# Transformer decoder layer, last stage: the output projection from f16 parts, and new instruction orders for four engines

## What is computed

```python
x = x + attention(layernorm(x)) @ Wo                       # 16 heads, short and long attention mixed
x = x + cross_attention(query=layernorm(x), memory=ctx)    # 8 heads, 77 memory rows, masked
x = x + fp4_linear(silu(fp4_linear(h, w_gate)) * fp4_linear(h, w_up), w_down)   # h = layernorm(x)
```

## Time and profile before

| | |
|---|---|
| median of 3 runs | 4975.11 us (4972.73 to 4979.94) |
| the profiled execution | 4978.72 us; its span 4976.8 us |
| mean granted TensorE clock | 0.981 |
| TensorE busy, whole span | 4782.2 us (96%) |
| VectorE, ScalarE, GpSimd busy | 4042.0 us (81%), 2998.2 us (60%), 3012.5 us (61%) |
| last stage, 3870 to 4977 us | TensorE 1030.65 us busy, VectorE 878.11, ScalarE 555.07, GpSimd 357.27; clock 0.95 |

### The profile page before, as it was taken

The page is one execution under the profiler, slowest core; times in us unless marked ns, Lnnn a source line. Parts: engine busy times, 40 slices in busy tenths (PEclk is TensorE's granted clock), DMA queues, the critical chain, the costliest instruction groups (busy, mean ns, idle before and its releaser), DMA issues. The chain is left out here.

```text
span 4976.8 us, 101555 instructions
## 1 busy us (share of the span) xinstructions
PE 4782.2 (96%) x31276; PEld 2096.8 (42%) x31276; DVE 4042.0 (81%) x6613; ACT 2998.2 (60%) x5234; POOL 3012.5 (61%) x1267
## 2 busy tenths in 40 slices
PE   6999899999999999999999999999998699999998
PEld 3444233333333333333333333333332477777776
DVE  6657888888888888888888888888884488888887
ACT  2222377777777767777776777777676355555554
POOL 0000388787888878878788888878788133333332
PEclk9999799999999999999999999999999699999999
DMA  4444467677676777767777676777766200000000
GB/s 151 139 124 128 108 171 169 174 167 179 168 171 168 172 175 170 170 168 172 175 169 173 167 173 172 169 175 167 176 157 148 67 20 26 26 27 27 26 22 12
DMA packets 216978, 661.83 MB, mean 133 GB/s; under 512 B 38099, under 2 KB 111955, under 8 KB 158997
## 3 DMA queue, kind: packets, MB, share of 16 engines
q0 software_dynamic: 64512, 469.79, 40.6%
q1 hardware_dynamic: 151957, 185.66, 12.5%
HBM read 123.56 MB, written 61.64 MB: 37 GB/s over the span
## 5 line engine op out<-in xcount | busy, mean ns | idle before, releaser
L874 DVE TENSOR_REDUCE rowmax_parts<-scores_qk 128x1 f32<-128x512 f32 x4096 | 2523.6, 678 | 462.9 <-PE scores_qk L947 462.9
L854 ACT ACTIVATE probs_T<-scores_kq 128x512 f32<-128x512 f32 x4096 | 2286.3, 596 | 978.6 <-PE scores_kq L947 915.2
L788 POOL TENSOR_TENSOR probs_added<-probs_added,probs_T 128x2048 f32<-128x2048 f32 x448 | 2030.3, 4532 | 458.3 <-ACT probs_T L854 446.9
L947 PE MATMUL scores_kq<-q_operand,k_operand 103*128 103x512 f16 (+3 forms) x3712 | 1274.5, 349 | 10.2 <-ACT probs_T L854 8.3
L947 PE MATMUL scores_qk<-k_operand,q_operand 96*128 96x512 f16 (+4 forms) x3712 | 1121.6, 351 | 43.2 <-DMA k_operand<-positions_dram 18.4
L1018 PE MATMUL outputs_T<-probs_T,v_operand 128*32 128x512 f32 x8192 | 1091.8, 605 | 1.3 <-ACT probs_T L854 1.3
L947 PEld LDWEIGHTS scores_kq<-q_operand,k_operand 103*128 103x128 f16 x3712 | 358.6, 97 | 920.5 <-ACT probs_T L854 635.4
L947 PEld LDWEIGHTS scores_qk<-k_operand,q_operand 96*128 96x128 f16 (+1 forms) x3712 | 354.8, 98 | 437.3 <-DVE rowmax_parts L874 184.4
L1624 PE MATMUL f_gate_up<-w_gate_up,xq_T 128*128 128x256 f16 (+1 forms) x4608 | 494.1, 265 | 8.6 <-DVE hidden L1515 7.5
L1624 PEld LDWEIGHTS f_gate_up<-w_gate_up,xq_T 128*128 128x128 f16 x4608 | 421.2, 98 | 77.8 <-issue 25.4
L788 POOL TENSOR_TENSOR probs_added<-probs_T 128x2048 f32<-128x2048 f32 x64 | 290.3, 4535 | 237.7 <-ACT probs_T L854 237.7
(11 more groups left out here) (165 smaller groups left out, 4296.2 us busy)
## 6 DMA issues: line engine op xcount, KB each, us to landing
probs_poured<-probs_T POOLq DMA_DIRECT2D x448, 1024.0 KB, 7.2
qk_parts_dram<-qk_parts SPq DMA_DIRECT2D x96, 256.0 KB, 2.9
q_operand<-qk_parts_dram SPq DMA_DIRECT2D x192, 128.0 KB, 2.6
k_operand<-qk_parts_dram SPq DMA_DIRECT2D x192, 128.0 KB, 3.1
v_dram<-v_heads SPq DMA_DIRECT2D x16, 1024.0 KB, 5.7
v_operand<-v_dram SPq DMA_DIRECT2D x64, 256.0 KB, 6.1
q_operand_above<-qk_parts_dram SPq DMA_DIRECT2D x96, 128.0 KB, 2.8
x_groups<-x SPq DMA_DIRECT2D x8, 1024.0 KB, 9.3
```

What stands on the lines that cost most here:

```text
L788: nc.gpsimd.tensor_tensor(total, first, probs[:, b % PBUF, :], ALU.add).then_inc(added.sem, 1)
L854: nc.scalar.activation(probs[:, kb % PBUF, qt * BANK:(qt + 1) * BANK], pb[:, k % 2, :], ACT.Exp)\
L874: nc.vector.reduce_max(rowmax[:, w % 2, c // NQ, c % NQ:c % NQ + 1], pa[:, k % 3, :], AX.X)\
L947: return nc.tensor.matmul(out, lhsT, rhs, start=start, stop=stop, skip_group_check=True)
```

## The change

Wo (scaled by 64) and each tile's attention outputs are split into f16 parts; "project" becomes 12 f16 matmuls instead of 4 in f32. Wo is split once, ahead of the tiles: high part on ScalarE, low part on VectorE. Two new entries split a tile: "high attn" (ScalarE) and "low attn" (GpSimd), both two tiles ahead; the buffer of the parts is single. "measure out" undoes the scaling. All four orders are new; tiles' offsets change too.

```diff
 ORDER_PE = (
-    ("turn h 0", -2), ("project", 1), ("ff2", -1), ("ff3", -1), ("turn h 1", -2), ("ff4", -1), ("turn q", 1),
-    ("turn h 2", -2), ("ff5", -1), ("down1", -2), ("logits", 1), ("down2", -2), ("turn x", 0), ("down0", -2),
-    ("ff1", 0), ("turn probs", 1), ("ff0", 0), ("cross", 1),
+    ("turn h 0", -2), ("turn probs", 0), ("ff0", -1), ("cross", 0), ("ff1", -1), ("project", 1), ("ff3", -1),
+    ("turn h 1", -2), ("ff2", -1), ("ff5", -1), ("down0", -2), ("turn h 2", -2), ("turn q", 1), ("ff4", -1),
+    ("logits", 1), ("down1", -2), ("down2", -2), ("turn x", 0),
 )
 ORDER_DVE = (
-    ("gate1", -1), ("gate0", -1), ("measure cross", 0), ("measure out", 1), ("shift cross", 0), ("scale x", 0),
-    ("gate2", -1), ("shift out", 1), ("gate3", -1), ("exponents x", 0), ("quantise h0", -1), ("gate5", -1),
-    ("gate4", -1), ("softmax", 1), ("quantise h1", -1), ("sum probs", 1), ("scale cross", 1), ("add down", -2),
+    ("quantise h1", -2), ("sum probs", 0), ("scale cross", 0), ("gate0", -1), ("gate1", -1),
+    ("measure cross", 0), ("measure out", 1), ("shift cross", 0), ("scale x", 0), ("gate3", -1),
+    ("shift out", 1), ("gate2", -1), ("exponents x", 0), ("quantise h0", -1), ("softmax", 1), ("gate4", -1),
+    ("gate5", -1), ("add down", -2),
 )
 ORDER_ACT = (
-    ("silu0", -1), ("high h1", -2), ("copy hT 0", -2), ("root cross", 0), ("root out", 1), ("norm cross", 0),
-    ("silu2", -1), ("silu3", -1), ("copy hT 1", -2), ("norm out", 1), ("copy hT 2", -2), ("copy q", 1),
-    ("silu4", -1), ("silu5", -1), ("high x", 0), ("copy xT", 0), ("exp", 1), ("copy probs", 1), ("high h0", -1),
-    ("silu1", 0),
+    ("exp", 0), ("copy xT", -1), ("copy probs", 0), ("silu0", -1), ("high h1", -2), ("copy hT 0", -2),
+    ("silu1", -1), ("root cross", 0), ("root out", 1), ("norm cross", 0), ("silu3", -1), ("silu2", -1),
+    ("high attn", 2), ("copy hT 1", -2), ("silu5", -1), ("norm out", 1), ("copy q", 1), ("copy hT 2", -2),
+    ("high x", 0), ("silu4", -1), ("high h0", -1),
 )
 ORDER_POOL = (
-    ("add cross", 0), ("low h1", -2), ("divide x", 0), ("round x", 0), ("low x", 0), ("low h0", -1),
+    ("low h0", -2), ("add cross", 0), ("low h1", -2), ("divide x", 0), ("round x", 0), ("low x", 0),
+    ("low attn", 2),
 )
...
+                if kind == "low attn":
+                    a_hi.passed(pool, n)
+                    nc.gpsimd.tensor_tensor(aT_parts[:, 1, :, :], aT[:, n % 2, :, :], aT_parts[:, 0, :, :], ALU.subtract)\
+                        .then_inc(a_lo.sem, 1)
...
+            act.wait_ge(weights, 64)
+            nc.scalar.activation(wo_parts[:, 0, :, :], wo_sb[:, :, :], ACT.Copy, scale=UPSCALE).then_inc(wo_hi, 1)
             act.wait_ge(ready, 3)
...
+                if kind == "high attn":
+                    got[n % 2].passed(act, n // 2)
+                    o_product.passed(act, n - 1)
+                    nc.scalar.copy(aT_parts[:, 0, :, :], aT[:, n % 2, :, :]).then_inc(a_hi.sem, 1)
...
+            dve.wait_ge(wo_hi, 1)
+            nc.vector.scalar_tensor_tensor(wo_parts[:, 1, :, :], wo_sb[:, :, :], UPSCALE, wo_parts[:, 0, :, :],
+                                           ALU.mult, ALU.subtract).then_inc(wo_lo, 1)
...
                 if kind == "measure out":
-                    nc.vector.tensor_tensor(x1[:, n % 2, :], pl[:, 0, :], xt[:, n % 2, :], ALU.add).then_inc(summed1.sem, 1)
+                    nc.vector.scalar_tensor_tensor(x1[:, n % 2, :], pl[:, 0, :], 1.0 / UPSCALE, xt[:, n % 2, :],
+                                                   ALU.mult, ALU.add).then_inc(summed1.sem, 1)
...
                 if kind == "project":
-                    got[n % 2].passed(pe, n // 2)
+                    if n == 0:
+                        pe.wait_ge(wo_lo, 1)
+                    a_lo.passed(pe, n)
                     x_scaled.passed(pe, n - 1)
                     for c in range(KT):
-                        last = nc.tensor.matmul(pl[:, 0, :], aT[:, n % 2, c, :], wo_sb[:, c, :], start=c == 0, stop=c == KT - 1)
+                        for a, b in PRODUCTS:
+                            last = nc.tensor.matmul(pl[:, 0, :], aT_parts[:, a, c, :], wo_parts[:, b, c, :],
+                                                    start=c == 0 and a == b, stop=c == KT - 1 and a == 1)
```

More of the change, by code:

```diff
@@ L1180, in finish @@
         wo_sb = sb("wo_sb", [P, KT, H], F32)
+        wo_parts = sb("wo_parts", [P, 2, KT, H], F16)
         wd = sb("w_down", [P, FT, 2, H], F16)
@@ L1192, in finish @@
         aT = sb("attn_T", [P, 2, KT, P], F32)
+        aT_parts = sb("attn_T_parts", [P, 2, KT, P], F16)
         x1 = sb("x1", [P, 2, H], F32)
@@ L1233, in finish @@
         M = lambda name, per=1, step=1: Mark(sem("f_" + name), per, step)
+        wo_hi, wo_lo = sem("f_wo_hi"), sem("f_wo_lo")
         weights, wd_in, k_turned, k_copied, mask_link, ident0, ready = (sem("f_" + k) for k in
@@ L1240, in finish @@
         shifted = [M(f"shifted{i}") for i in range(2)]
+        a_hi, a_lo = M("attn_hi"), M("attn_lo")
         o_product, summed1, q_turned, q_copied = M("o_product"), M("x1"), M("q_turned"), M("q_copied")
@@ L1304, in slot @@
             def slot(kind, n):
-                if kind == "add cross":
+                if kind == "low attn":
+                    a_hi.passed(pool, n)
+                    nc.gpsimd.tensor_tensor(aT_parts[:, 1, :, :], aT[:, n % 2, :, :], aT_parts[:, 0, :, :], ALU.subtract)\
+                        .then_inc(a_lo.sem, 1)
+                elif kind == "add cross":
                     x_scaled.passed(pool, n)
@@ L1362, in slot @@
             def slot(kind, n):
-                if kind == "warm silu":
+                if kind == "high attn":
+                    got[n % 2].passed(act, n // 2)
+                    o_product.passed(act, n - 1)
+                    nc.scalar.copy(aT_parts[:, 0, :, :], aT[:, n % 2, :, :]).then_inc(a_hi.sem, 1)
+                elif kind == "warm silu":
                     warm(0, ACT.Silu)
```

## The result

The changed kernel takes 4988.39 us (median, 10 runs), the kernel before 4976.38 (10 runs): ratio 1.0025, 95% interval 1.0018 to 1.0033. It is 12 us slower; the forecast was 27 us slower.

What follows compares the result with a forecast made beforehand. The prediction took a loop (project, two ff pieces, VectorE from gate3 to `x_out`, project) as the bound. Loop 14, clock 9 and ends 4 made +27 on 4975, so 5002; own range 4988 to 5016, with rivals 4938 to 5028.

Steps and rivals of the forecast that it cites:

- The loop's +14: Last stage's loop of project, two ff pieces and VectorE from gate to `x_out`: 32.38 against 31.92, +0.46 a period, 14 us.
- the clock's "+9": TensorE's granted clock dropping to half in the last stage: 22 us of such falls against 13 before, +9, ends 0 and +32.
- Together +4: Start and end of the last stage: filling +2 and draining +2, estimates, ends -2 and +9.
- Rival 1: Last stage: TensorE is the bound and gets faster, neither new VectorE catch happens; 4924 to 4940, chance 0.18.
- rival 2: Last stage: one of two new VectorE catches (waits for GpSimd, in L112 or softmax's subtraction) fails; about 4976, chance 0.14.
- rival 3: Last stage: the clock falls to half in every period, +32 in place of +9; 5025, chance 0.18.
- rival 4: Project on TensorE: f16 parts save nothing, 0.91 a period more; 5029, chance under 0.01.
- the estimate that the prediction made of them: VectorE's new catches: 115 ns after release would make both 0.26 longer each, the sum some 15 us more; not adopted.
- two waits in disguise: VectorE in the old loop: L111 (1.80 against 0.96) and L113 on 640 columns (2.27 against 0.82) wait for GpSimd.
- falls in half of the periods: TensorE's clock at half in half of the periods, before one in 3.6: 15 falls of 1.5 us, 22 us.
- Filling, forecast +2: Ahead of the first project: splits of Wo and a tile's own two in series, partly offset by shorter projects; +2.
- Draining: End of the stage: "add down" of tile 30 ahead of quantise h1 of tile 31, waiting for down pieces; +2.

Runs made afterwards that it cites:

- run 1: Changed kernel with "low attn" moved behind "low h1" on GpSimd, "high attn" ahead of "root cross", the parts' buffer doubled: 4951.02 us, ratio to before 0.9951.
- run 2: Changed kernel with "high h0" and "low h0" put behind quantise h1, turn h 0 and turn h 1 later on TensorE: 4955.32 us, ratio to before 0.9962.
- run 4: Kernel before with the f16 parts added in its old orders, "low attn" behind "low h1" on GpSimd: 4942.49 us, ratio 0.9939.
- run 5: Changed kernel with the new orders only: project in f32, nothing split, no "high attn" or "low attn": 4977.39 us, ratio to before 1.0004.
- run 3: Changed kernel with "low attn" behind "low h1", "low h0" behind quantise h1, and no turn h between project and ff2: 4920.77 us, ratio to before 0.9891.
- run 6: Changed kernel with four f16 matmuls per tile, read by nothing, added on TensorE behind "turn x": 4972.53 us, ratio to before 0.9994.
- run 7: Kernel before with four f16 matmuls per tile, read by nothing, added on TensorE between turn h 0 and project: 4961.16 us, ratio 0.9971.

## Where the prediction was right, and which step failed

- **What failed.** The forecast was +27 and the measurement +12. The loop's +14 came as +11.6. The two terms beside it were mis-sized: the clock's "+9" measured +1.9, and "Together +4" for filling and draining measured -2.9, with the wrong sign.
- **The loop was right:** +0.46 forecast, +0.40 measured (32.32 against 31.92), 11.6 us over 29 periods against 14. Each term is in the rows: project 2.59; L112 +0.83 for 0.84; the subtraction +0.86 for 0.92; quantise h1 free. Runs 1, 2, 4 and 5 take out one part of the change each, run 3 both catches and a turn; each period comes within 0.15 of its sum. Rival 1 (TensorE the bound), rival 2 (a catch fails), rival 3 (a fall in every period: ten in 29) and rival 4 (f16 saves nothing: project 2.59) fell.
- **The lock.** The rule of the Trainium skill ("SBUF — State Buffer", section "SBUF: two separate sides") holds here: L112 takes 1.79 us beside "low attn" and 0.96 without. The 115 ns of the same page of the Trainium skill (section "A bandwidth-pool intuition that's wrong (but worth ruling out)") were measured on a blocked DMA, and no run here blocks one; the estimate that the prediction made of them for VectorE did not come true: L112 ended 0.81 after release, as L111 had in the earlier trace rows.
- **More catches than two.** The prediction counted two waits in disguise in the loop of before. L108 (two SBUF inputs) and L109 (one) on 768 columns are delayed as well: GpSimd's "round x" runs beside them, from 4438.36 to 4441.36. VectorE before, the same steady period, and below it the last tile, when GpSimd is idle:

```profile
4438.84 1.60 DVE L108 SCALAR_TENSOR_TENSOR hidden_q<-hidden,f_inv 128x768 f32<-128x768 f32 x1
4440.48 1.30 DVE L109 TENSOR_SCALAR f_m<-hidden_q 128x768 uint32<-128x768 uint32 x1
```

```profile
4945.94 0.96 DVE L108 SCALAR_TENSOR_TENSOR hidden_q<-hidden,f_inv 128x768 f32<-128x768 f32 x1
...
4946.93 0.56 DVE L109 TENSOR_SCALAR f_m<-hidden_q 128x768 uint32<-128x768 uint32 x1
```

With L111 that is some 2.2 us in a period. They stand in the changed kernel too (1.60, 1.30 and 1.80), so the forecast difference is not touched; no run here removes them.

- **"falls in half of the periods", +9: wrong in size.** The forecast had 15 falls of 1.5 in 30 periods. About 10 of 1.51 in 29 came, against 7.6 of 1.70 before: +1.9. That idle time among transposes has to do with them was right in kind: filled with matmuls, it brings hardly any in runs 6 and 7. (Whether the idle time counts or the missing matmul work, these runs do not tell apart.) How often they come cannot be read from the length of a wait alone: with 1.05 and 0.78 us of waits there are ten, with 0.19 and 0.78 none in the steady part, and none with 1.23 us in run 2, while 0.92 in the kernel before brought about eight. What sets their number stays open.
- **"Together +4" for filling and draining: wrong in sign.** Filling, forecast +2, was -4.05. The forecast took the splits of Wo and the longer start, but no clock: run 7, with the orders of before, gains 5 us there by filler alone, so what the forecast took as given, the clock in the filling of the kernel before, was itself a loss. Why the filling of the changed kernel is shorter isn't told apart by these runs; the parts alone gave 2.0 us, the orders alone 5.5, and the two don't add. Draining was +1.15 for +2: right in kind, since "add down" of tile 30 now waits ahead of quantise h1 of tile 31:

```profile
4964.49 0.69 DVE L1549 SCALAR_TENSOR_TENSOR y_out<-f_down,x 128x512 f32<-128x512 f32 x1 [3.03 <-PE f_down L1633]
```

- **The sum.** 14 + 9 + 4 = 27 against 11.6 + 1.9 - 2.9, less 0.8 ahead of the stage: 9.8 between the profiled executions, 12 between the medians. The mechanism of the loop carried the sign, and two terms for whose size no row stood doubled the amount. That the 4988 measured still touches the low end of the forecast's own range owes to the width of that range.
- **What neither part alone shows.** The parts alone are 32 us faster, the orders alone the same (+1.6); together they are 12 us slower. The changed order puts "low attn" where VectorE is caught and brings the waits behind which the clock falls: run 1 moves that one operation (with "high attn" ahead of it and a second buffer) and takes off 37 us.

## What to carry to other kernels

Before counting saved time on the busiest engine, close the period: find instructions whose start-to-start distances add up to it exactly. Only what lies on that loop counts, and a GpSimd operation set beside a VectorE operation with two SBUF inputs lies on it. Give such GpSimd work the stretches in which VectorE reads PSUM, reduces or takes statistics; one SBUF input alone is no safe sign, as L109 shows.

## What was not expected of the hardware

Work that nobody reads made both kernels faster: four f16 matmuls per tile in idle time took 15 us off the kernel before (4976 to 4961) and 16 off the changed one, and the granted clock hardly fell any more (falls 1.8 and 0.8 us). And the falls shrank far more than the waits that they follow: 14.9 us of falls with waits of 1.05 and 0.78 us in a period, 1.9 us in run 1 with 0.21 and 0.78, all of it in the first of the 29 periods.
